# Where the edge-counting units stand between the matmul units of a graph layer: two passes later in the Q loop, and spread by another rule behind the O and neighbour units

## The chip, the cores and the metric

The kernel runs on one core of a Trainium2 chip. The metric is device time in microseconds (us). Before the change the median of three runs is 1108.72 us (1108.17 to 1108.83).

TensorE (PE in the rows) does the matmuls, with its weight loads as PEld. VectorE (DVE) and ScalarE (ACT) take results out of PSUM, the buffer that matmuls write to. GpSimd (POOL) and SyncE (SP) do little here: SP issues the weight loads from memory.

## The reference

A layer of a graph network on 625 nodes with 1024 features and 20000 edges, all in fp32:

```
xn = layernorm(x)
x  = x + sage(xn, src, dst) + linear_attention(xn)
x  = x + moe(layernorm(x))

sage, one layer:  agg = segment_sum(h[src], dst)
                  h @ W_self + (agg / deg) @ W_neigh + b      (two layers, relu between)
attention:        q = softmax(x Wq, features) / 8;  k = softmax(x Wk, tokens)
                  context = k^T v;  out = (q context) Wo + bo     (16 heads of 64)
```

The sum over edges is done as a product with a count matrix C (source node by target node). The kernel builds C from the edge list on the chip. The mixture of experts after it (8 experts, 2 per token, and a shared one) isn't touched by the change.

## The kernel before, in words

**Precision.** Each fp32 product is made of three passes of a "hi" part and a "lo" part: hi*hi, hi*lo, lo*hi (lines 1653 to 1655). Weights are split when they have landed: ScalarE casts `w_hi` (line 688), then VectorE subtracts for `w_lo` (line 996), a quarter of a matrix at a time.

**Units and the ring.** All work of TensorE is cut into units, listed in one order in `units` (lines 97 to 150). Unit number n in that list writes PSUM buffer n mod 4 (`RING = 4`, `slot`). Before a unit starts, `claim` waits until the unit four places ahead of it in the list has been taken out of that buffer. ScalarE or VectorE gives the buffer back (`free`). A unit's place in the list is thus also what decides for whom it waits. Each engine's own program runs in order.

**Names.** In the texts here a unit is called by its kind and number:
- q0 to q9: the query projection of token tile m mod 5, half m // 5, of 24 matmuls. VectorE takes it: maximum (line 1318), subtraction (1323, which gives the buffer back), then ScalarE's exponential (798), VectorE's sum (1327), reciprocal and scaling (1331).
- qt0 to qt9: the transposes of a normalised q tile (line 1692), two passes later (`QLAG = 2`). ScalarE copies them out (802).
- at0 to at4: attention of a token tile (line 1818): 8 matmuls in 16 rows. ScalarE casts `at_hi` (776), VectorE makes `at_lo` (1307) and then gives the buffer back.
- ctx0, ctx1: the attention context (1784).
- o(h,i) and g0(h,i): the output projection and the neighbour projection, half h, token tile i. They are in `mains`, 20 units. VectorE adds the bias to o (1357). For g0 ScalarE casts the hi part (692) and VectorE makes the lo part (1002) and gives the buffer back.
- c0 to c48: counting units. Each is four small matmuls (line 1752) of two one-hot matrices. ScalarE makes `src_oh` (785 four times, then 788), VectorE makes `dst_oh` (1276). VectorE adds the result into C (1288, twice) and gives the buffer back (1290). Three sets of one-hots are kept (`GBUF = 3`): set u+3 is made after unit c(u) is done.
- hs0, hs1, ...: the node's own projection in the first graph layer, after the mains.

**Order of the Q loop.** It has passes m = 0 to 11. TensorE issues q(m), then qt(m-2), then the counts of `Q_COUNTS[m]`, then the at units of `BEHIND_QT[m]` (8: at0, 9: at1, 10: at2, 11: at3 and at4). Before, `Q_COUNTS` puts c0 to c7 in passes 0 to 7, one each. VectorE's pass is: the softmax of q(m); `context` in passes 0 and 1; a weight split in passes 0, 1, 6 and 7; the adding of the pass's count and the next one-hot; the `at_lo`. So a weight split stands ahead of the count's adding. ScalarE's pass is: exponential, copy of qt(m-2), the `w_hi` of passes 0, 1, 6, 7, the `src_oh`, the `at_hi`.

**Order of the mains.** Behind each of the 20 units stand its counts (`behind`): two each, and three behind o(0,3), together 41. Weight splits stand at token tiles 1 and 2 of each half.

Of the kernel before, what the change touches and what calls it, by code (L numbers as in the profile page):

```python
# [5 lines left out]
def gps_layer(nc, x, src, dst, w_self0, w_neigh0, b0, w_self1, w_neigh1, b1,  # L6
# [26 lines left out]
    NT = -(-N // T)  # L33
# [32 lines left out]
    CU = NG // PER  # L66
# [37 lines left out]
    BEHIND_QT = {2 * NT - 2: [0], 2 * NT - 1: [1], 2 * NT: [2], 2 * NT + 1: [3, 4]}  # L104
    for m in range(KF + KLAG - 1):
        units += ([("k", m)] if m < KF else []) + ([("kt", m - KLAG)] if m >= KLAG else []) + ([("perm", m - 1)] if m else [])
    Q_COUNTS = {m: [m] for m in range(2 * NT - QLAG)}
    IN_Q = len(Q_COUNTS)
    BEHIND_Q = {0: [("kt", KF - 1), ("ctx", 0)], 1: [("ctx", 1)]}
    for m in range(2 * NT + QLAG):  # L110
        if m < 2 * NT:
            units += [("q", m)] + BEHIND_Q.get(m, [])
        if m >= QLAG:
            units += [("qt", m - QLAG)]
        units += [("cnt", u) for u in Q_COUNTS.get(m, [])]
        units += [("at", i) for i in BEHIND_QT.get(m, [])]
    mains = [(name, h, i) for name in ("o", "g0") for h in range(2) for i in range(NT)]
    SPLIT_AT = {1: 0, 2: 1}
    behind = {key: 2 for key in mains}
    behind[("o", 0, NT - 2)] += CU - IN_Q - 2 * len(mains)  # L120
    assert behind[("o", 0, NT - 2)] in (1, 2, 3)
    mixed, u = [], IN_Q
    for m, key in enumerate(mains):
        mixed.append(key)
        for _ in range(behind[key]):
            mixed.append(("cnt", u))
            u += 1
    assert u == CU
# [74 lines left out]
    with ctx:  # L203
# [470 lines left out]
        def _(act):  # L674
            copy = nc.scalar.copy

            def wait_unit(key, base=None):
                act.wait_ge(ready[slot(key)], use(key) + 1 if base is None else base * BU + (use(key) + 1))

            def split_hi(job, base=None, quarters=(0, 1)):  # L680

                b = job % 2
                shift = (lambda v, per: v) if base is None else (lambda v, per: base * per + v)
                if job >= 2:
                    wait_unit(last_unit[job - 2], base)
                for s in quarters:
                    act.wait_ge(w_loaded[s], shift(16 * (job + 1), 64))
                    copy(w_hi[b][:, s * HK:(s + 1) * HK, :], w_raw[s][:, :, :]).then_inc(hi_done, 1)  # L688
# [103 lines left out]
            for m in range(2 * NT + QLAG):  # L792
# [13 lines left out]
                if m in Q_SPLITS:  # L806
                    split_hi(Q_SPLITS[m][0], quarters=Q_SPLITS[m][1:])
                for u in Q_COUNTS.get(m, []):
                    wait_unit(("cnt", u))
# [176 lines left out]
        def _(dve):  # L986
# [19 lines left out]
            def wait_unit(key, base=None):  # L1006
                dve.wait_ge(ready[slot(key)], use(key) + 1 if base is None else base * BU + (use(key) + 1))
# [213 lines left out]
            for m in range(KF):  # L1221
                key, b = ("k", m), m % 2
# [90 lines left out]
            for m in range(2 * NT + QLAG):  # L1313
                if m < 2 * NT:
                    key, rows = ("q", m), R(m % NT)
                    q_b = q_s[0:rows, m % 2, :]
                    wait_unit(key)
                    V_.reduce_max(q_m[0:rows, :], heads(PS(key)[0:rows, 0, :]), axis=AX.X)
                    V_.drain()
                    if m >= 2:  # L1320

                        dve.wait_ge(ready[slot(("qt", m - 2))], use(("qt", m - 2)) + 1)
                    V_.tensor_tensor(heads(q_b), heads(PS(key)[0:rows, 0, :]), wide(q_m[0:rows, :]),
                                     ALU.subtract).then_inc(q_sub, 1)
                    V_.drain().then_inc(free[slot(key)], 1)
                    dve.wait_ge(q_expd, m + 1)
                    V_.reduce_sum(q_sum[0:rows, :], heads(q_b), axis=AX.X)
                    V_.drain()
                    V_.reciprocal(q_sum[0:rows, :], q_sum[0:rows, :])
                    V_.drain()  # L1330
                    V_.scalar_tensor_tensor(heads(q_b), heads(q_b), float(DH) ** -0.5,
                                            wide(q_sum[0:rows, :]), ALU.mult, ALU.mult).then_inc(q_done, 1)
                    if m < 2:
                        context(m)
                    if m in Q_SPLITS:
                        split_lo(Q_SPLITS[m][0], quarters=Q_SPLITS[m][1:])
                if m == 0:
                    dve.wait_ge(bin_at_ready, 1)
                    dve.wait_ge(c_cleared, 1)
                bins_at = load_bins(Q_COUNTS.get(m, []))  # L1340
                for u in Q_COUNTS.get(m, []):
                    add_counts(u, bins_at)
                    one_hots(u + GBUF)
                for i in BEHIND_QT.get(m, []):
                    attention_lo(i)
# [92 lines left out]
            for n in range(KF):  # L1438
                if n == HK:
                    split_lo(J_L1)  # L1440
                key = ("h", n)
# [19 lines left out]
            for h in range(2):  # L1461
                split_lo(J_L1 + 2 * h + 1)
                for i in range(NT):
                    key = ("g1", h, i)
# [7 lines left out]
                for i in range(NT):  # L1472
                    key = ("x1", h, i)
# [136 lines left out]
            with dve.Fori(0, blocks) as j:  # L1610
                for h in range(2):
                    split_lo(J_X + h + 1, j)
                    for n in range(h * HK // 2, (h + 1) * HK // 2):
                        key = ("he", n)
# [25 lines left out]
        def _(pe):  # L1640
# [181 lines left out]
            for m in range(2 * NT + QLAG):  # L1822
# [10 lines left out]
                if m >= QLAG:  # L1833
                    n = m - QLAG
                    pe.wait_ge(q_done, n + 1)
                    transposes(("qt", n), lambda a: q_s[0:R(n % NT), n % 2, a * 128:(a + 1) * 128], HK, R(n % NT), R(n % NT))
                for u in Q_COUNTS.get(m, []):
                    count(u)
# [279 lines left out]
```

## Time and profile before

| | |
|---|---|
| median of three runs | 1108.72 us |
| the profiled execution's own time | 1108.72 us |
| its span, first to last instruction | 1106.7 us |
| TensorE busy | 1092.8 us, 99% of the span |
| VectorE, ScalarE busy | 639.7 us (58%), 483.1 us (44%) |
| passes of the Q loop | from 146.73 us (q0) to 230.23 us (start of o(0,0)) |
| mains and their counts | 230.23 to 354.79 us (start of hs0) |
| granted clock | 1.00 |

A timeline row gives the start in us, the duration in us, engine, line, operation, output<-input, shapes, how many are merged, and in brackets how long the engine was idle before it and who released it. Matmul records overlap: the next matmul starts before the record of the one ahead of it ends. So the distance of two starts is the price of a step, and the idle time in brackets understates a stall by the part that the record ahead covers. A weight-load row is a matmul's companion and isn't shown.

### The profile page before, as it was taken

To read this page: it belongs to the slowest core of one execution; us is meant where nothing else is said; L and a number is where in the kernel's file an instruction comes from. 1 tells how busy PE (TensorE), PEld (TensorE's weight loads), DVE (VectorE), ACT (ScalarE), POOL (GpSimd) and SP (SyncE) were. 2 spreads that over 40 slices of the span, in tenths; PEclk is the share of its full clock that TensorE was granted. 3 is DMA by queue.
4 is the path that set the end of the run, shared out by engine and by line. 5 is a ranking of instruction groups with operands and counts; after the bars stand their busy time and mean duration, and the time that the engine had idled before them with its cause. 6 is when DMAs were issued, how large, how long until landed. Compare 5 with 4: busy or idle time off the path is not lost.

```text
span 1106.7 us, 16447 instructions
## 1 busy us (share of the span) xinstructions
PE 1092.8 (99%) x6225; PEld 948.2 (86%) x6225; DVE 639.7 (58%) x880; ACT 483.1 (44%) x712; POOL 67.2 (6%) x88
## 2 busy tenths in 40 slices
PE   7999999999999999999999999999999999999998
PEld 5889998787778999878789999898888988988876
DVE  6889967755666753343474423444746656556556
ACT  4513344557786321301234222245655646555550
POOL 2000000000000000000000530200000000000003
PEclk9999999999999999999999999999999999999999
DMA  7222202213322103622004442477577576766757
GB/s 250 77 77 77 72 9 74 76 58 117 111 77 77 60 19 120 219 76 76 1 1 169 154 111 77 151 258 271 175 270 251 195 277 218 236 228 208 238 182 283
DMA packets 76488, 157.01 MB, mean 142 GB/s; under 512 B 7160, under 2 KB 7432, under 8 KB 76432
## 3 DMA queue, kind: packets, MB, share of 16 engines
q1 hardware_dynamic: 64908, 127.30, 34.0%
q10 hardware_dynamic: 7300, 15.41, 3.8%
q0 software_dynamic: 4224, 13.55, 3.8%
q8 instruction: 36, 0.59, 0.2%
q14 instruction: 20, 0.16, 0.0%
HBM read 135.69 MB, written 20.54 MB: 141 GB/s over the span
## 4 chain that ended last, share of the span: by engine, by line
PE 88%; DVE 4%; ACT 2%; DMA 2%; DVEq 2%; issue 1%; SPq 0%; POOL 0%; ACTq 0%; POOLq 0%
PE ps L1653 21%; PE ps L1655 21%; PE ps L1654 21%; PE ps L2067 10%; PE ps L2068 5%; PE ps L1692 1%; PE ps L1738 1%; PE ps L1970 1%; PE ps L1901 1%; PE ps L1971 1%; PE ps L1902 1%; DVE x L1631 1%; PE ps L1752 1%; ACT src_oh L785 1%; ACT w_hi L688 1%
## 5 line engine op out<-in xcount | busy, mean ns | idle before, releaser
L996 DVE TENSOR_TENSOR w_lo<-w_raw,w_hi 128x2048 fp32r<-128x2048 f32 x108 | 245.2, 2290 | 137.5 <-ACT w_hi L688 135.5
L688 ACT CAST w_hi<-w_raw 128x2048 fp32r<-128x2048 f32 x108 | 203.8, 1911 | 96.6 <-PE ps L1971 36.2
L2067 PE MATMUL ps<-xe,w_hi 128*128 128x448 f32 x512 | 160.9, 375 | 0.0
L2068 PE MATMUL ps<-xe,w_lo 128*128 128x224 f32 x512 | 134.8, 263 | 0.0
L2067 PEld LDWEIGHTS ps<-xe,w_hi 128*128 128x128 f32 x512 | 95.9, 187 | 7.9
L1653 PE MATMUL ps<-w_hi,he_hi 128*128 128x512 f32 (+1 forms) x256 | 101.2, 395 | 0.0
L1655 PE MATMUL ps<-w_hi,he_lo 128*128 128x512 f32 (+1 forms) x256 | 100.2, 391 | 0.0
L1654 PE MATMUL ps<-w_lo,he_hi 128*128 128x512 f32 (+1 forms) x256 | 100.0, 391 | 0.0
L1653 PE MATMUL ps<-w_hi,xt_hi 128*128 128x512 f32 (+1 forms) x240 | 95.9, 400 | 2.1 <-DVEq L1290 2.0
L2068 PEld LDWEIGHTS ps<-xe,w_lo 128*128 128x128 f32 x512 | 97.5, 190 | 0.4
L1655 PE MATMUL ps<-w_hi,xt_lo 128*128 128x512 f32 (+1 forms) x240 | 93.7, 390 | 0.0
L1654 PE MATMUL ps<-w_lo,xt_hi 128*128 128x512 f32 (+1 forms) x240 | 93.6, 390 | 0.0
L1653 PE MATMUL ps<-xt_hi,w_hi 128*128 128x314 f32 x256 | 79.4, 310 | 0.0
L1653 PE MATMUL ps<-t_hi,w_hi 128*128 128x314 f32 x256 | 78.8, 308 | 0.0
L1654 PE MATMUL ps<-t_lo,w_hi 128*128 128x314 f32 x256 | 78.8, 308 | 0.0
L1655 PE MATMUL ps<-xt_hi,w_lo 128*128 128x314 f32 x256 | 78.7, 307 | 0.0
L1655 PE MATMUL ps<-t_hi,w_lo 128*128 128x314 f32 x256 | 78.6, 307 | 0.0
L1654 PE MATMUL ps<-xt_lo,w_hi 128*128 128x314 f32 x256 | 78.6, 307 | 0.0
L785 ACT ACTIVATE src_oh<-iota_c,src_f 128x128 f16<-128x128 bf16 x196 | 62.4, 389 | 20.3 <-DVE o_s L1357 15.3
L1653 PE MATMUL ps<-w_hi,t_hi 128*128 128x512 f32 (+1 forms) x160 | 62.6, 391 | 0.0
L1655 PE MATMUL ps<-w_hi,t_lo 128*128 128x512 f32 (+1 forms) x160 | 62.4, 390 | 0.0
L1654 PE MATMUL ps<-w_lo,t_hi 128*128 128x512 f32 (+1 forms) x160 | 62.4, 390 | 0.0
(324 smaller groups left out, 1986.7 us busy)
## 6 DMA issues: line engine op xcount, KB each, us to landing
w_raw<-in_L_ffn_w SPq DMA_DIRECT2D x64, 1024.0 KB
w_raw<-in_L_gnn_W_neigh SPq DMA_DIRECT2D x8, 1024.0 KB
w_raw<-in_L_gnn_W_self SPq DMA_DIRECT2D x8, 1024.0 KB
w_raw<-in_L_ffn_shared_gate_up SPq DMA_DIRECT2D x8, 1024.0 KB
w_raw<-in_L_mix_Wv SPq DMA_DIRECT2D x4, 1024.0 KB
w_raw<-in_L_mix_Wk SPq DMA_DIRECT2D x4, 1024.0 KB
w_raw<-in_L_mix_Wq SPq DMA_DIRECT2D x4, 1024.0 KB
w_raw<-in_L_mix_Wo SPq DMA_DIRECT2D x4, 1024.0 KB
```

The source lines that it names most:

```text
L688: copy(w_hi[b][:, s * HK:(s + 1) * HK, :], w_raw[s][:, :, :]).then_inc(hi_done, 1)
L785: nc.scalar.activation(src_oh[b][:, c, :], iota_c[:, 0:128, 0], ACT.Abs, bias=src_f[:, g * GC + c:g * GC + c + 1]).then_inc(src_abs, 1)
L996: V_.tensor_tensor(w_lo[b][:, k, :], w_raw[s][:, :, :], as32(w_hi[b][:, k, :]), ALU.subtract).then_inc(lo_done, 1)
L1631: V_.scalar_tensor_tensor(x1[0:R(i), i, :], y_g[c][0:R(i), i, :], wts[0:R(i), c, i:i + 1], x1[0:R(i), i, :], ALU.mult, ALU.add)
L1653: mat(out_ap, lh, rh, start=start, stop=False)
L1654: mat(out_ap, lh, rl, start=False, stop=False)
L1655: return mat(out_ap, ll, rh, start=False, stop=stop)
L1692: last = nc.tensor.transpose(PB(key)[:, a * width:(a + 1) * width], source(a), ident[0:ins, 0:ins])
L1738: last = mat(PB(key)[:, 0:LC], by_place[u % 2][0:rows, n // IL * 128:(n // IL + 1) * 128, n % IL], by_column[u % 2][0:rows, n // IL * LC:( ...
L1752: last = mat(PS(key)[:, a, 0:TD], src_oh[b][:, a * CG + c, :], dst_oh[b][:, a * TD:(a + 1) * TD, c], start=c == 0, stop=c == CG - 1)
L2067: mat(PS(key)[:, a, 0:2 * B], wh[:, k, w_cols], xe[:, :, k, 0:B], start=k == 0, stop=False)
L2068: last = mat(PS(key)[:, a, 0:B], wl[:, k, w_cols], xe_hi[:, k, 0:B], start=False, stop=k == KF - 1)
```

## The change

Two tables of places are made in another way. Nothing is computed differently.

```diff
-    Q_COUNTS = {m: [m] for m in range(2 * NT - QLAG)}
+    Q_COUNTS = {m: [m - QLAG] for m in range(QLAG, 2 * NT)}
...
-    behind = {key: 2 for key in mains}
-    behind[("o", 0, NT - 2)] += CU - IN_Q - 2 * len(mains)
-    assert behind[("o", 0, NT - 2)] in (1, 2, 3)
+    weights_to = [sum(1.75 if key[2] in SPLIT_AT else 2.25 for key in mains[:m + 1]) for m in range(len(mains))]
     mixed, u = [], IN_Q
     for m, key in enumerate(mains):
         mixed.append(key)
-        for _ in range(behind[key]):
+        while u < IN_Q + int((CU - IN_Q) * weights_to[m] / weights_to[-1]):
             mixed.append(("cnt", u))
             u += 1
...
-                if m == 0:
+                if m == QLAG:
                     dve.wait_ge(bin_at_ready, 1)
                     dve.wait_ge(c_cleared, 1)
```

**Q loop.** c0 to c7 now stand in passes 2 to 9, in place of passes 0 to 7. Passes 0 and 1 have none. In passes 8 and 9 a count now stands between qt and at, on TensorE, on VectorE and on ScalarE. VectorE's waits for the cleared C move with the first count.

**Mains.** The number of counts behind each unit, in the order of the units:

| | o(0,0..4) | o(1,0..4) | g0(0,0..4) | g0(1,0..4) |
|---|---|---|---|---|
| before | 2 2 2 3 2 | 2 2 2 2 2 | 2 2 2 2 2 | 2 2 2 2 2 |
| now | 2 2 1 3 2 | 2 2 2 2 2 | 2 2 2 2 2 | 3 1 2 2 3 |

In the rows that follow, `psum_free2` is the semaphore of buffer 2, and line numbers of the changed kernel are lower by 2.

TensorE in pass 8, from qt6 (`ident,q_s`) over at0 (`q_first`, `q_second` with `ctx_s`) to q9 (`w_hi_50,xt_hi`), before:

```order
L1692 MATMUL ps<-ident,q_s 128x128 [waits psum_free1,q_done]
L1692 MATMUL ps<-ident,q_s 128x128 x3
L1818 MATMUL ps<-q_first,ctx_s 128x128 [waits psum_free2,qt_done,ctx_done]
L1818 MATMUL ps<-q_first,ctx_s 128x128 x3
L1818 MATMUL ps<-q_second,ctx_s 128x128 x4
L1653 MATMUL ps<-w_hi_50,xt_hi 113x512 [waits psum_free3]
```

and now:

```order
L1690 MATMUL ps<-ident,q_s 128x128 [waits psum_free3,q_done]
L1690 MATMUL ps<-ident,q_s 128x128 x3
L1750 MATMUL ps<-dst_oh_128,src_oh_131 128x157 [waits src_ready,oh_ready,psum_free0]
L1750 MATMUL ps<-dst_oh_128,src_oh_131 128x157 x3
L1816 MATMUL ps<-q_first,ctx_s 128x128 [waits psum_free1,qt_done,ctx_done]
L1816 MATMUL ps<-q_first,ctx_s 128x128 x3
L1816 MATMUL ps<-q_second,ctx_s 128x128 x4
L1651 MATMUL ps<-w_hi_50,xt_hi 113x512 [waits psum_free2]
```

The count c6 stands ahead of at0, and at0 claims buffer 1, which c5 of pass 7 had; q9 claims buffer 2, which q8 had. Before, at0 claimed the buffer of qt5 and q9 that of the count c7.

VectorE in pass 8, from the maximum of q8 to `at_lo` of at0 and the maximum of q9, before:

```order
L1318 TENSOR_REDUCE q_m<-ps 128x8 [waits psum_ready0]
L1323 TENSOR_TENSOR q_s<-ps,q_m 128x512 [waits psum_ready1]
L1327 TENSOR_REDUCE q_sum<-q_s 128x8 [waits q_expd]
L1329 RECIPROCAL q_sum<-q_sum 128x8
L1331 SCALAR_TENSOR_TENSOR q_s<-q_s,q_sum 128x512
L1307 TENSOR_TENSOR at_lo<-ps,at_hi 128x4x128 [waits hi_out] x2
L1318 TENSOR_REDUCE q_m<-ps 113x8 [waits psum_ready3]
```

and now, from the sum of q8 (its maximum and subtraction stand ahead as before) to `at_lo` of at0:

```order
L1325 TENSOR_REDUCE q_sum<-q_s 128x8 [waits q_expd]
L1327 RECIPROCAL q_sum<-q_sum 128x8
L1329 SCALAR_TENSOR_TENSOR q_s<-q_s,q_sum 128x512
L1294 TENSOR_LOAD bin_at
L1294 ISA x4
L1286 ISA [waits psum_ready0]
L1286 TENSOR_TENSOR c_f<-c_f,ps 128x157
L1286 ISA
L1286 TENSOR_TENSOR c_f<-c_f,ps 128x157
L1274 TENSOR_TENSOR dst_oh_128<-iota_n,dst_126 128x628
L1305 TENSOR_TENSOR at_lo<-ps,at_hi 128x4x128 [waits hi_out] x2
```

The loading of two column offsets, two additions into `c_f` and a one-hot stand ahead of `at_lo`.

TensorE behind g0(1,0), from the first count to g0(1,1) (`w_hi_50,xt_hi`), before:

```order
L1752 MATMUL ps<-dst_oh_128,src_oh_131 128x157 [waits src_ready,oh_ready,psum_free2]
L1752 MATMUL ps<-dst_oh_128,src_oh_131 128x157 x3
L1752 MATMUL ps<-dst_oh_129,src_oh_132 128x157 [waits src_ready,oh_ready,psum_free3]
L1752 MATMUL ps<-dst_oh_129,src_oh_132 128x157 x3
L1653 MATMUL ps<-w_hi_50,xt_hi 128x512 [waits psum_free0]
```

and now:

```order
L1750 MATMUL ps<-dst_oh_130,src_oh_133 128x157 [waits src_ready,oh_ready,psum_free1]
L1750 MATMUL ps<-dst_oh_130,src_oh_133 128x157 x3
L1750 MATMUL ps<-dst_oh_128,src_oh_131 128x157 [waits src_ready,oh_ready,psum_free2]
L1750 MATMUL ps<-dst_oh_128,src_oh_131 128x157 x3
L1750 MATMUL ps<-dst_oh_129,src_oh_132 128x157 [waits src_ready,oh_ready,psum_free3]
L1750 MATMUL ps<-dst_oh_129,src_oh_132 128x157 x3
L1651 MATMUL ps<-w_hi_50,xt_hi 128x512 [waits psum_free0]
```

g0(1,0) itself had buffer 1 before and has buffer 0 now. So g0(1,1) claims the buffer of g0(1,0), where it claimed the buffer of a count ahead of g0(1,0). The same holds for hs0 behind g0(1,4).

## Rows read from the trace of the kernel before

**Rows 1.** The page: TensorE's line of busy time, and its granted clock.
```profile
PE 1092.8 (99%) x6225; PEld 948.2 (86%) x6225; DVE 639.7 (58%) x880; ACT 483.1 (44%) x712; POOL 67.2 (6%) x88
...
PEclk9999999999999999999999999999999999999999
```

**Rows 2.** Waits of TensorE, whole span: who, for whom, total us, times, longest.
```profile
PE ps L1653 <- DVEq L1290: 2.0, 3, 0.9
```

**Rows 3.** Timeline of TensorE near 174 us: start, duration, instruction, idle before.
```profile
173.84 0.45 PE L1752 MATMUL ps<-dst_oh,src_oh 128*128 128x157 f16 x4
175.06 0.50 PE L1653 MATMUL ps<-w_hi,xt_hi 128*128 128x512 f32 x1 [0.77 <-DVEq L1290]
```

**Rows 4.** Timeline of VectorE, same place.
```profile
171.79 2.29 DVE L996 TENSOR_TENSOR w_lo<-w_raw,w_hi 128x2048 fp32r<-128x2048 f32 x1 [0.21 <-issue]
...
174.60 0.32 DVE L1288 TENSOR_TENSOR c_f<-c_f,ps 128x157 f32 x1 [0.17 <-issue]
```

**Rows 5.** Timeline of TensorE, 213 to 231 us.
```profile
213.34 1.06 PE L1818 MATMUL ps<-q_first,ctx_s 128*128 128x128 f32 x8
214.24 1.06 PE L1818 MATMUL ps<-q_second,ctx_s 128*128 128x128 f32 x8
215.58 0.49 PE L1653 MATMUL ps<-w_hi,xt_hi 128*113 128x512 f32 x1 [0.29 <-DVEq L1290]
...
226.67 1.13 PE L1818 MATMUL ps<-q_first,ctx_s 128*128 128x128 f32 x8 [0.17 <-DVEq L1309]
...
230.23 0.48 PE L1653 MATMUL ps<-w_hi,at_hi 128*128 128x512 f32 x1
```

**Rows 6.** Timeline of VectorE, 212 to 226 us.
```profile
212.45 2.29 DVE L996 TENSOR_TENSOR w_lo<-w_raw,w_hi 128x2048 fp32r<-128x2048 f32 x1 [0.82 <-ACT w_hi L688]
...
216.78 0.69 DVE L1323 TENSOR_TENSOR q_s<-ps,q_m 128x512 f32<-128x512 f32 x1
...
221.39 0.69 DVE L1318 TENSOR_REDUCE q_m<-ps 113x8 f32<-113x512 f32 x1 [0.29 <-PE ps L1655]
...
225.19 1.28 DVE L1307 TENSOR_TENSOR at_lo<-ps,at_hi 128x512 fp32r<-128x512 f32 x2
```

**Rows 7.** Timeline of VectorE, one pass of the Q loop with a count.
```profile
175.49 0.69 DVE L1318 TENSOR_REDUCE q_m<-ps 128x8 f32<-128x512 f32 x1
...
181.33 0.69 DVE L1318 TENSOR_REDUCE q_m<-ps 128x8 f32<-128x512 f32 x1
```

**Rows 8.** Timeline of ScalarE at 224 us.
```profile
224.09 1.07 ACT L776 CAST at_hi<-ps 128x512 fp32r<-128x512 f32 x2
```

**Rows 9.** Timeline, 250 to 257 us: TensorE three, ScalarE three, VectorE one.
```profile
254.56 0.75 PE L1752 MATMUL ps<-dst_oh,src_oh 128*128 128x157 f16 x8
256.34 0.45 PE L1752 MATMUL ps<-dst_oh,src_oh 128*128 128x157 f16 x4 [1.03 <-ACT src_oh L788]
256.58 0.47 PE L1653 MATMUL ps<-w_hi,at_hi 128*113 128x512 f32 x1
...
250.61 1.91 ACT L688 CAST w_hi<-w_raw 128x2048 fp32r<-128x2048 f32 x1 [0.27 <-issue]
...
253.73 0.63 ACT L788 ACTIVATE src_oh<-src_oh 128x512 f16<-128x512 f16 x1
...
255.56 0.63 ACT L788 ACTIVATE src_oh<-src_oh 128x512 f16<-128x512 f16 x1
...
255.40 0.69 DVE L1357 TENSOR_TENSOR o_s<-ps,bias_o 128x512 f32<-128x512 f32 x1
```

**Rows 10.** Timeline near 330 us: TensorE, VectorE.
```profile
329.89 0.74 PE L1752 MATMUL ps<-dst_oh,src_oh 128*128 128x157 f16 x8
...
330.70 0.69 DVE L1002 TENSOR_TENSOR n_lo<-ps,n_hi 128x512 fp32r<-128x512 f32 x1 [2.33 <-ACT n_hi L692]
```

**Rows 11.** Timeline of TensorE at the start of the program.
```profile
5.00 4.93 PE L1760 MATMUL ps<-iota_c 128*128 128x392 bf16 x19 [5.00 <-POOLq L588]
...
11.34 1.99 PE L1760 MATMUL ps<-iota_c 128*128 128x392 bf16 x11
```

## The prediction

> **What bounds the kernel now.** I read the page first: TensorE is busy for 1092.8 of 1106.7 us, and the clock row holds 9 in all 40 slices [rows 1]. So the time is TensorE's work plus its stalls. A count that is moved costs the same matmuls wherever it stands; the change is worth only the stalls that it removes or makes. The waits of TensorE come next: in the stretch that the change touches it waited three times for VectorE to give back the buffer of a count, 2.0 us together [rows 2], and once for ScalarE's one-hots [rows 9]. So I then read the timelines at these places, and for each claim in the new order asked when its buffer comes free.
>
> The profiled execution took 1108.72 us, 2.0 us more than its span, and is equal to the median. The sum is made on it. Distances are from start to start; a release reaches TensorE 0.14 us after VectorE's last addition ends (174.60 + 0.32 = 174.92, TensorE at 175.06) [rows 3, 4]. A count alone takes TensorE 0.24 us, two take 0.54, so three take 0.81 (256.34 to 256.58; half of 0.54 for one more) [rows 9]. Where I replay the new order I stay on the old trace's time axis and shift nothing until the end.
>
> **Part 1, the start of the Q loop (c0, c1 out of passes 0 and 1).** q3 should start 0.24 after c2, at 174.08, and started at 175.06: 0.98 lost, waiting for c1, whose adding stood behind the weight split of pass 1 (171.79 to 174.08) [rows 3, 4]. Now q3 claims the buffer of ctx1, which VectorE gives back ahead of that split. The stall goes: **-0.98**. What is late next is nothing: q4 claims c0, which VectorE adds in pass 2, and a pass of VectorE with a count takes 5.84 us (175.49 to 181.33) [rows 7], less than TensorE's own, so it has caught up. The edit to the wait for the cleared C costs nothing, it only moves later.
>
> **Part 2, passes 6 and 7.** q8 claims c4 where it claimed c6. Both are added in pass 6 behind its weight split, so this stall stays: 0.
>
> **Part 3, at0 and q9.** c6 stands ahead of at0, which so wants to start at 213.34 + 0.24 = 213.58 [rows 5]. It claims the buffer of c5, which VectorE adds in pass 7, behind the weight split of 212.45 to 214.74 [rows 6]. In the old trace the count of that pass was released to q9 at 215.58, and VectorE's pass is unchanged. So at0 starts at 215.58: +2.00. It takes 2 * 0.90 = 1.80 (213.34 to 214.24 is its half) and ends at 217.38. q9 claims q8, given back at the end of the subtraction: 216.78 + 0.69 + 0.14 = 217.61 [rows 6], so +0.23. The old stall of q9 goes, 215.58 - (214.24 + 0.90) = 0.44. Together **+1.79**. Behind the waiting at0 stand q9 and all the rest of TensorE's program. q9 starts at 217.61.
>
> **Part 4, passes 8 to 11.** VectorE took up q9 5.81 us after its start (215.58 to 221.39) [rows 5, 6], now at 223.42. Pass 9 now holds a count, so `at_lo` of at1 starts after a whole pass of 5.84 [rows 7], at 229.26, takes 1.28 [rows 6] and ends at 230.54. ScalarE's extra one-hot set doesn't make it later: `at_hi` of at1 stood 2.70 after VectorE's maximum of q9 (224.09 - 221.39) [rows 6, 8] and moves by the 1.83 of a set (253.73 to 255.56) [rows 9]; its first half is ready 5.1 after the maximum, before 5.84. at3 claims the buffer of at1: 230.54 + 0.14 = 230.68. From at3 to the first output unit took 3.56 (226.67 to 230.23) [rows 5], now 234.24. That is 4.01 later than 230.23. Of it 0.48 is the two counts, which are work taken out of passes 0 and 1 and no loss, and 1.79 is part 3. The rest is **+1.74**, stalls at qt9 (which claims c7) and at3. Cover: at4 and its casts move along with at3; the bias load is issued after at4, and the weight loads of SP follow splits that are not reordered. Bounds: nothing lost (0, if `at_lo` kept its old distance to q9), and 3.6 if the two sets of ScalarE, 2 * 1.83, came on the path whole. I take 1.74, from the pass row, since VectorE's chain is the longer one.
>
> **Part 5, behind o(0,3).** Before, the third count c16 should have started at 254.56 + 0.54 and started at 256.34, waiting for a one-hot set ready at 255.56 + 0.63 = 256.19; o(0,4) then at 256.58 [rows 9]. Now o(0,2) has one count, the third one behind o(0,3) is c15, and its set is the one ready at 253.73 + 0.63 = 254.36, in time. What is late next is the buffer: three counts behind a unit make the next unit claim that unit's own buffer. VectorE's split has to wait for `w_hi`, 250.61 + 1.91 = 252.52, ends at 254.81, and the bias addition ends at 255.50, released 255.64. o(0,4) starts there, 0.94 earlier, of which 0.27 is the count that is still to come: **-0.67**. Bounds: 0, if one wait only takes the place of the other, and -1.24, if both are gone (256.34 against 255.10). The replay names both ends of the wait, so I take it.
>
> **Part 6, behind g0(1,0) and g0(1,4).** Each now has three counts, so g0(1,1) claims g0(1,0) and hs0 claims g0(1,4). It wants to start 0.81 after 329.89, at 330.70. VectorE starts the lo part only then, because ScalarE's cast goes ahead, and releases at 330.70 + 0.69 + 0.14 = 331.53 [rows 10]: 0.83 lost. The second place has the same pattern. Together **+1.66**. Bounds: 0, if the lo part came before the third count ended, and 2.0 with a restart of 0.1 to 0.2 each. The last counts end a little later, but the casting of C is wanted only after hs1, 14 us on.
>
> **Sum.** -0.98 + 1.79 + 1.74 - 0.67 + 1.66 = +3.54. After hs0 TensorE waited for one thing only in the rest of the program, so the shift is carried to the end unchanged. 1108.72 + 3.54 = **1112.3 us**.
>
> By the Trainium skill ("Perfetto Trace Analysis", Optimizing Tensor Performance) independent matmul groups rotated through different PSUM banks let the evacuation of one overlap the next group's matmuls. Taken as it stands, part 6 would be 0. The trace agrees for two counts behind a unit (the waits of TensorE name none behind any pair in the mains, which takes 0.54), and limits it for three: the rotation hides an evacuation only if it is shorter than the units ahead of the next use, here 0.81 against 1.64.
>
> **The rivals.**
> - *Faster (the other side).* VectorE gives the moved counts' buffers back in time. Then the stalls of q3 (0.98), q9 (0.44) and c16 (1.24) go and none comes: 1108.72 - 2.7 = 1106.0. For it: VectorE has 42% of its time free. Against it: in pass 7 the split is ahead of c5's adding. It decides at 213.58; the split alone ends at 214.74 [rows 6]. This would need VectorE 2.0 us ahead there.
> - *The Q loop's tail hides the two late counts.* Part 4 is 0: 1110.5. For it: before, the two `at` units behind pass 9 lost only some tenths. Against it: at3's claim hangs on VectorE's pass 9, which is longer by the count.
> - *The counts by three cost nothing.* Part 6 is 0: 1110.6. Against it: rows 10.
> - *The clock falls.* Stalls of up to 2 us follow each other in passes 8 to 11. The same constant matmul took 0.26 us on average at the program's start and 0.18 in its second group [rows 11], 1.44 times; the granted clock reads 1.00 (2.4 GHz) in both. If the 15 us from q9 to the first output unit went by that ratio, 6.6 more: 1118.9. Against it: no dip in any slice after stalls of 1 us [rows 1, 9]. The Trainium skill ("TensorE: Matmul & The Clock Gate", A second HAM failure mode: psum-queue depth-cycling) tells of a kernel in which short waits between groups for PSUM made the clock swing; no stretch of this trace shows it.
>
> **How the numbers follow.** Forecast 0.82 (1112.3); tail hidden 0.06; counts by three free 0.05; faster 0.05; clock 0.02. What a measurement can tell from no change is about 0.2%, 2.2 us. The forecast and the clock are slower by more: 0.84. The two cases of +1.8 and +1.9 are within: 0.11. Faster: 0.05. The range goes from just under the two cases in which one part fails (1110.4) to the forecast with the restarts and half of part 4's upper bound (+1.4), 1113.7.
>
> **What would show it.** In the changed kernel's waits of TensorE: no wait at q3; one of about 1.8 at at0 (line 1816) for a count's adding, one at qt9 of about 0.8 and one at at3 over 1 us; none for one-hots at the third count; one of some 0.6 at each of g0(1,1) and hs0 for the lo part. o(0,0) starts near 232.8 in place of 230.23, hs0 near 358.4 in place of 354.79. A start of o(0,0) before 231 would break parts 3 and 4, and with them the forecast.

## The result: slower, and by more than forecast

| | before | changed |
|---|---|---|
| median | 1108.72 us (1108.17 to 1108.84, 5 runs) | 1115.33 us (1112.98 to 1119.59, 5 runs) |
| ratio of the runs | | 1.0069 [1.0042, 1.0097] |
| profiled execution, span | 1108.72, 1106.7 us | 1114.83, 1112.7 us |

The forecast was 1112.3 us, and 1110.4 to 1113.7 as its range. The direction was right. The time lies 3.0 us above the forecast and outside the range. In most comparisons of this case, for the kernel before too, some runs are 4 us or more longer than the rest.

The changed kernel's page: TensorE's busy time and its granted clock in tenths, for [rows 1].

```profile
PE 1095.3 (98%) x6225; PEld 950.0 (85%) x6225; DVE 639.5 (57%) x880; ACT 482.8 (43%) x712; POOL 68.3 (6%) x88
...
PEclk9999999999999999999999999999999999999999
```

The same 6225 matmuls are busy for 2.5 us longer. Busy time alone doesn't say why: mains_only below, in whose windows the clock never falls, has 1.0 more than the kernel before, since the record ahead of each new stall runs into it. The clock row has slices of 28 us and hides a short fall; the windows further down show one.

TensorE's waits in the changed kernel, whole span (who, for whom, us in total, times, longest), for [rows 2]:

```profile
...
PE ps L1816 <- DVEq L1288: 1.9, 1, 1.9
PE ps L1651 <- DVEq L1002: 1.6, 3, 0.7
PE ps L1651 <- DVEq L1357: 1.4, 1, 1.4
PE ps L1816 <- DVEq L1307: 1.2, 1, 1.2
PE ps L1651 <- DVEq L1288: 0.9, 1, 0.9
PE ps L1690 <- DVEq L1288: 0.7, 1, 0.7
```

From top to bottom: at0 waits for a count's adding; g0(1,1), hs0 and a place of 0.4 that the kernel before has too; o(0,4) for its neighbour's bias addition; at3 for at1; q8 as before; qt9 for a count. No wait for one-hots is left.

TensorE's timeline at q3, at q8, around at0 and q9, and through the loop's tail, for [rows 3, 5]; the last line is VectorE's subtraction of q8:

```profile
173.20 0.45 PE L1750 MATMUL ps<-dst_oh,src_oh 128*128 128x157 f16 x4
173.44 0.47 PE L1651 MATMUL ps<-w_hi,xt_hi 128*128 128x512 f32 x1
...
205.68 0.50 PE L1651 MATMUL ps<-w_hi,xt_hi 128*128 128x512 f32 x1 [0.92 <-DVEq L1288]
...
214.04 1.13 PE L1816 MATMUL ps<-q_first,ctx_s 128*128 128x128 f32 x8 [1.89 <-DVEq L1288]
215.01 1.67 PE L1816 MATMUL ps<-q_second,ctx_s 128*128 128x128 f32 x8
216.33 0.77 PE L1651 MATMUL ps<-w_hi,xt_hi 128*113 128x512 f32 x1
...
217.75 0.63 PE L1651 MATMUL ps<-w_hi,xt_hi 128*113 128x512 f32 x1
218.18 0.63 PE L1652 MATMUL ps<-w_lo,xt_hi 128*113 128x512 f32 x1
...
218.88 0.40 PE L1651 MATMUL ps<-w_hi,xt_hi 128*113 128x512 f32 x1
...
223.02 0.60 PE L1690 MATMUL ps<-ident,q_s 128*128 128x128 f32 x4
...
228.71 0.58 PE L1690 MATMUL ps<-ident,q_s 113*128 113x113 f32 x4 [0.69 <-DVEq L1288]
230.53 1.13 PE L1816 MATMUL ps<-q_first,ctx_s 128*128 128x128 f32 x8 [1.24 <-DVEq L1307]
...
215.14 0.69 DVE L1321 TENSOR_TENSOR q_s<-ps,q_m 128x512 f32<-128x512 f32 x1
```

q3 follows its count after 0.24 us, without a wait: part 1. at0 waits 1.89: part 3. Then the same eight matmuls that take 1.06 in [rows 5] take 1.67, and those of q9 start 0.43 apart (217.75 to 218.18) where 0.23 is usual, until 218.88. So q9 takes 6.69 (216.33 to 223.02) against 5.61 in the kernel before (215.58 to 221.19). Below, qt9 and at3 wait as part 4 has it.

The granted clock in stretches (us, TensorE busy, instructions, clock, DMA share, GB/s), changed kernel:

```profile
213.00:216.00 3.00, 1.96 (x14) 0.88 0.60 140
216.00:219.00 3.00, 3.00 (x11) 0.55 0.54 210
219.00:222.00 3.00, 3.00 (x15) 1.00 0.00 0
```

1.00 is 2.4 GHz and 0.50 would be 1.2 GHz, so TensorE ran most of 216 to 219 us at the lower level. Before, all these stretches read 1.00. The cost: 0.35 in at0's second half and 1.08 in q9, together 1.4. q9 started at 216.33 and was due at 215.98: the halves of at0 stand 0.97 apart, and q8's buffer, which q9 claims, came free at 215.14 + 0.69 + 0.14 = 215.97.

The Trainium skill ("TensorE: Matmul & The Clock Gate", A second HAM failure mode: psum-queue depth-cycling) tells of a matmul loop whose short waits for PSUM made the clock swing. The prediction weighed a fall of the clock and gave it 2 in 100. This trace agrees in part: the clock fell behind a wait for PSUM, but once, for some 3 us, behind a single wait of 1.89, and it didn't swing.

VectorE at the second place, 255 to 260 us, for [rows 9]; then TensorE there and at the two places of part 6:

```profile
256.56 2.29 DVE L994 TENSOR_TENSOR w_lo<-w_raw,w_hi 128x2048 fp32r<-128x2048 f32 x1 [0.70 <-ACT w_hi L686]
259.76 0.69 DVE L1355 TENSOR_TENSOR o_s<-ps,bias_o 128x512 f32<-128x512 f32 x1 [0.91 <-issue]
```

```profile
258.16 1.03 PE L1750 MATMUL ps<-dst_oh,src_oh 128*128 128x157 f16 x12
260.64 0.46 PE L1651 MATMUL ps<-w_hi,at_hi 128*113 128x512 f32 x1 [1.45 <-DVEq L1357]
...
333.94 1.03 PE L1750 MATMUL ps<-dst_oh,src_oh 128*128 128x157 f16 x12
335.55 0.50 PE L1651 MATMUL ps<-w_hi,xt_hi 128*128 128x512 f32 x1 [0.58 <-DVEq L1002]
...
359.16 1.03 PE L1750 MATMUL ps<-dst_oh,src_oh 128*128 128x157 f16 x12
360.87 0.38 PE L1651 MATMUL ps<-xt_hi,w_hi 128*128 128x314 f32 x1 [0.68 <-DVEq L1002]
```

The split had waited for `w_hi`, which part 5 had in its sum. Behind it stand 0.91 us marked "issue", which it had not: before, the split waited for nothing and the bias addition followed at once (255.40) [rows 9]:

```profile
253.14 2.28 DVE L996 TENSOR_TENSOR w_lo<-w_raw,w_hi 128x2048 fp32r<-128x2048 f32 x1
```

Start times by segment, changed less before: q8 -1.63; q8 to o(0,0) +5.50; o(0,0) to o(0,4) +0.19; o(0,4) to hs0 +2.02. Sum +6.08, against +6.11 in time.

### The profile page after: what moved, and what is told of

Read it like the earlier page. It is cut to its first block, busy times and chain, and to the rows that moved or that the text cites. A ratio compares the mean times of both kernels' runs of the same rounds, so it can differ in the third digit from the quotient of the medians.

```text
span 1112.7 us, 16447 instructions
## 1 busy us (share of the span) xinstructions
PE 1095.3 (98%) x6225; PEld 950.0 (85%) x6225; DVE 639.5 (57%) x880; ACT 482.8 (43%) x712; POOL 68.3 (6%) x88
## 4 chain that ended last, share of the span: by engine, by line
PE 90%; DVE 4%; DMA 2%; ACT 2%; DVEq 1%; issue 1%; POOL 0%; SPq 0%; ACTq 0%; POOLq 0%
PE ps L1651 21%; PE ps L1653 21%; PE ps L1652 21%; PE ps L2065 10%; PE ps L2066 5%; PE ps L1690 1%; PE ps L1736 1%; PE ps L1968 1%; PE ps L1899 1%; PE ps L1969 1%; PE ps L1900 1%; DVE x L1629 1%; PE ps L1782 1%; PE ps L1750 1%; ACT w_hi L686 1%
```

## The experiments

Each ran in up to twelve timed runs on one chip beside the kernel before, whose median there was 1108.9 to 1109.1. "Mean clock" is that of a whole run. A fall of 3 us takes about 0.0015 off it, so it shows as 0.998 or 0.999. It doesn't say where in the run the clock fell, and the kernel before too has 0.998 in 11 of its 123 runs, so it is a weaker witness than the windows of a profile. The lowest run is given beside the median.

### Each half of the change alone

q_only has `Q_COUNTS` of the changed kernel and the mains of the one before; mains_only the reverse.

```
-    Q_COUNTS = {m: [m] for m in range(2 * NT - QLAG)}
+    Q_COUNTS = {m: [m - QLAG] for m in range(QLAG, 2 * NT)}
```

> The Q loop's part of the change alone; the mains as before. Theory (stalls by claims, and a clock that falls after the stall of 1.9 us at at0): -0.98 at q3, +1.79 at at0 and q9, +1.74 in the tail, that is +2.5 us: 1111.2 where the granted clock stays at 1.00; in most runs it falls after at0 and the run is 1.5 us or more longer, with a spread between runs of several us as in the changed kernel. Rival (the clock has nothing to do with at0; the mains' stalls bring the spread): all runs within 1 us of 1111.2 and mean clock 1.000 in all.

> The mains' part of the change alone; the Q loop as before. Theory: o(0,4) waits for its own buffer (+0.4 against the old one-hot wait, as the changed kernel's trace shows, where the forecast had -0.67), g0(1,1) and hs0 0.8 each: +2.0 us, 1110.7, all runs within 0.5 us and mean clock 1.000, as no stall is over 1.7 us. Rival (the mains bring the spread): runs from 1110 to 1116 with clocks under 1.

q_only: median 1112.65, lowest 1110.40, no run with a mean clock of 1.000 and six of twelve at 0.998 or less. mains_only: 1110.70, lowest 1110.12, ten of twelve at 1.000. Windows of q_only:

```profile
213.00:216.00 3.00, 2.10 (x11) 0.70 0.64 166
216.00:219.00 3.00, 3.00 (x14) 0.73 0.47 184
...
231.00:234.00 3.00, 3.00 (x18) 0.55 0.02 5
234.00:237.00 3.00, 3.00 (x19) 0.88 0.04 11
...
965.00:968.00 3.00, 3.00 (x13) 0.53 0.88 335
```

mains_only agrees with its expectation in the median; three of its runs lie more than 0.5 above, which it had excluded. q_only has the waits of its sum (1.9, 0.7 and 1.2 at at0, qt9 and at3); its median lies 1.4 above the sum, in the direction of a fallen clock, but its lowest run 0.8 below it, which stays unexplained. The falls belong to the Q loop's part: one behind at0, and in this profile a second behind qt9 and at3. A third stands far from the change, behind a wait of 1.98 us for the experts' weights (the matmul that waited starts at 963.61).

### A stall of a chosen length ahead of at0

Three kernels add one wait of TensorE to the kernel before, at the place where the changed kernel stalls, and move nothing.

```
                 pe.wait_ge(qt_done, NT + i + 1)
+                if i == 0:
+                    pe.wait_ge(lo_done, 14)                 # dose_short
+                    pe.wait_ge(q_sub, 9)                    # dose_long
+                    pe.wait_ge(free[slot(("cnt", 7))], use(("cnt", 7)) + 1)   # dose_count7
```

> The kernel before with one wait more: at0 also waits for the weight split of pass 7 (ends 214.74 in the old trace, at0 wants 213.34), one stall of about 1.5 us. Theory (a fall of the clock needs a single stall near 2 us or more): +1.1 us (the old stall of q9 goes), 1109.8, clock 1.000 in all runs. Rival (stalls near 1 us add up to a fall whenever they stand close): falls in some runs, up to 1112 and more.

> The kernel before with one wait more: at0 also waits for VectorE's subtraction of q8, given at 217.5 in the old trace: one stall of about 4.1 us. Theory (a single long stall brings the fall): +3.7 us for the stall, and the clock falls in every run, 1.5 us or more on top: 1113.9 or more. Rival (the fall needs the several stalls of the changed kernel's passes 8 to 11): 1112.4, clock 1.000.

> The kernel before with one wait more: at0 waits until the count of pass 7 has been added, which is what it waits for in the changed kernel by the ring of buffers. Its stall is about 2.1 us (213.34 to 215.58, less the count), between the 1.5 of dose_short, after which the clock was 1.00 in all runs, and the 4.2 of dose_long, after which it fell in all. Without a fall: +2.2 at at0, -0.3 at q9, 1110.6. Theory A (one stall of about 2 us right behind that of q8 is enough): the granted clock falls below 0.9 at 216 to 222 us in most runs, mean clock under 0.9995, and they take 1 to 3 us more, 1111.5 to 1113.5. Theory B (only the later stalls at qt9 and at3 together with it bring the clock down in the changed kernel): the clock stays 1.00 and the time is 1110.6.

| | stall at at0 | median, lowest us | runs with a mean clock of 0.998 or less |
|---|---|---|---|
| dose_short | 1.5 | 1110.05, 1109.31 | 0 of 12 |
| dose_count7 | 2.3 | 1111.71, 1110.22 | 4 of 12 |
| dose_long | 4.2 | 1114.58, 1113.65 | 12 of 12 |

Windows of dose_long (those of dose_short and of the profiled run of dose_count7 read 1.00):

```profile
216.00:219.00 3.00, 1.30 (x10) 0.93 0.87 322
219.00:222.00 3.00, 3.00 (x12) 0.50 0.06 22
```

A stall by itself can bring the clock down: that of dose_long is a wait added to the kernel before, and nothing else was moved. dose_count7 was a miss for both theories: "most runs" was expected by one, none by the other. Three of its four low-clock runs take 1116.6 us or more, so they may have lost it elsewhere.

### The loop's late counts, one at a time

All three kernels keep six counts, behind passes 2 to 7, as in the changed kernel; two of them have a seventh. The extra counts of the mains stand behind units that are followed by no split.

```
+    Q_COUNTS = {m: [m - QLAG] for m in range(QLAG, 2 * NT - QLAG)}                # loop_2_to_7
+    Q_COUNTS = {2: [0], 3: [1], 4: [2], 5: [3], 6: [4], 7: [5], 9: [6]}           # loop_with_pass_9
+    Q_COUNTS = {2: [0], 3: [1], 4: [2], 5: [3], 6: [4], 7: [5], 8: [6]}           # loop_with_pass_8
```

> The kernel before with six counts in the Q loop, behind passes 2 to 7, as the changed kernel has them there, and none behind passes 8 and 9; third counts behind o(1,0), o(1,4) and g0(1,0), none behind o(0,3). It takes from the changed kernel's Q loop the two late counts alone. Theory A (each wait belongs to its place, as in parts 1, 3 and 4): no wait at q3, 0.9 at q8, nothing at at0, 0.3 at q9, nothing over 0.3 at qt9 and at3, 0.2 at o(1,1) and g0(0,0), 0.6 at g0(1,1); no fall of the clock at 213 to 237 us; 1108.7 - 1.0 - 1.2 + 0.15 + 0.2 + 0.6 = 1107.4. Theory B (moving all six counts two passes later makes VectorE late at the end of the loop whatever stands behind passes 8 and 9): at0 or at3 wait over 1 us, and the time is over 1109.

> As loop_2_to_7, with one count more in the Q loop, behind pass 9 (the changed kernel's second late count, without its first), and without the third count behind g0(1,0). It prices part 4 apart from part 3, and asks whether the loop's tail can bring the clock down by itself. Theory A (part 4 is the count of pass 9 alone): no wait at at0, 0.7 at qt9 and 1.2 at at3; against loop_2_to_7 +1.7 for the tail and -0.6 for g0(1,1): 1108.5 where the clock stays; and since its stalls of 0.7 and 1.2 are each shorter than the 1.5 after which it stayed, the mean clock is 1.000 or 0.999. Theory B (two stalls 1.8 us apart count together for the clock): it falls at 231 to 237 us in most runs, and they take about 1 us more, 1109.5. Theory C (part 4 was the echo of the stall at at0): qt9 and at3 wait under 0.5 each, 1107.0.

> As loop_with_pass_9, with the seventh count behind pass 8 in place of pass 9: the changed kernel's first late count without its second. Against loop_2_to_7 and loop_with_pass_9 it prices part 3 alone, and asks whether the stall at at0, without the later ones, brings the clock down. Theory A (part 3 is a matter of the claim alone): 1.9 at at0, none at q9 over 0.2, under 0.3 at qt9 and at3; lowest runs 1109.7, as those of loop_with_pass_9, since 1.8 there stands against 0.7 + 1.2 here. The clock: its stall (1.9, 0.9 at q8 six us ahead) lies between 1.5, after which the clock stayed, and 2.3, after which 4 of 12 runs had 0.998 or less; so it falls in a third of the runs at most. Theory B (the fall in the changed kernel comes from the stall at at0 and nothing else): a mean clock of 0.998 or less in most runs, as in q_only (all of 12 under 1.000).

TensorE's waits of loop_with_pass_9, then of loop_with_pass_8:

```profile
PE ps L1818 <- DVEq L1309: 1.2, 1, 1.2
...
PE ps L1692 <- DVEq L1290: 0.7, 1, 0.7
```

```profile
PE ps L1818 <- DVEq L1290: 1.9, 1, 1.9
```

Each wait goes with its own count, to a tenth: 1.9 at at0 with pass 8's (part 3), 0.7 and 1.2 at qt9 and at3 with pass 9's (part 4), and neither in loop_2_to_7, where at0 and qt9 don't wait and at3 waits 0.2 as before. Lowest runs: 1107.48, 1109.63 and 1110.03, against 1107.4, 1108.5 and 1109.7 expected. The one of pass 9 missed by a wait that it had not named, 0.7 for a one-hot set in the mains; that of pass 8 has such a wait too, of 1.0. The medians are far higher: 1115.27, 1113.00 and 1114.96. So the waits are read from the profiles, and the times bear on them only by the lowest runs; the long runs come back at the end.

The clock: with pass 8's count nine of twelve runs have a mean clock of 0.998 or less, with pass 9's two of twelve; of the runs under 1113 us, four of six and one of six. Windows of loop_with_pass_8 and of loop_with_pass_9:

```profile
213.00:216.00 3.00, 2.27 (x13) 0.70 0.60 180
216.00:219.00 3.00, 3.00 (x13) 0.73 0.44 170
```

```profile
216.00:219.00 3.00, 3.00 (x15) 1.00 0.46 178
...
231.00:234.00 3.00, 3.00 (x15) 1.00 0.73 236
```

So the stall at at0 brings it down without the later two. My expectation of "a third of the runs at most" was wrong, and theory B held. And dose_count7, with a longer stall there (2.3), kept its clock in most of its runs: four of twelve at 0.998 or less, one of the eight under 1113 us. So it looks as if the length of the stall alone doesn't decide, though twelve runs a kernel are few for that; what else does is open.

### What VectorE did in the 0.91 us ahead of the bias addition

hoist_load loads the next unit's column offsets ahead of the split instead of behind it. load_in_two leaves them in place but loads the third count's two offsets just ahead of its adding. Both are made from mains_only.

```
...
+                if key != mains[-1]:                                               # hoist_load
+                    bins_next = load_bins(counts_behind[mains[mains.index(key) + 1]])
                 if key[2] in SPLIT_AT:
                     split_lo(next_job(key), quarters=(SPLIT_AT[key[2]],))
```

```
-                bins_at = load_bins(counts_behind[key])                            # load_in_two
+                bins_at = load_bins(counts_behind[key][:2])
...
+                    if n == 2:
+                        bins_at += load_bins([u])
                     add_counts(u, bins_at[PER * n:PER * n + PER])
```

> The kernel before with the changed kernel's placing of the counts behind the main units (as mains_only), and in VectorE's program the loading of a unit's column offsets moved ahead of the weight split of the unit before it. It tells what held VectorE between the split of o(0,2) and the bias addition of o(0,3), where mains_only shows 0.91 us of idle time marked issue, and TensorE a wait of 1.7 us at o(0,4). Theory A (the loading of six offsets stands there; my part 5 took it at nothing): the bias addition follows the split at once, as in the kernel before; TensorE's wait at o(0,4) falls from 1.7 to about 0.8; the time is 0.9 below mains_only, 1109.8 against its 1110.7; the waits at g0(1,1) and hs0 stay. Theory B (the idle time belongs to the addition itself, restarting after a split that waited for ScalarE): the gap and the wait of 1.7 stay, and the time is 1110.7.

> As mains_only (the kernel before with the changed kernel's placing behind the main units), with VectorE's six column offsets of a unit with three counts loaded in two parts: four at the unit's start, two ahead of the third adding. hoist_load and five_in_the_loop show the loading of six offsets as 3.2 us of VectorE's sequencer (2.92 and 2.71 idle, with 0.3 beside the instruction before), or 0.53 an offset. Theory A (it is paid by the offset, and hidden as far as the split of 2.29 us lasts): four offsets take 2.1, less than 2.29, so the bias addition follows the split of o(0,2) at once, the wait at o(0,4) falls from 1.7 to 0.8, and about 1 us of idle time stands ahead of the third adding, which nobody waits for; 0.9 less than mains_only, 1109.8. Theory B (it is a fixed price for each loading that follows a waiting split): the gap of 0.9 and the wait of 1.7 stay, 1110.7.

VectorE in hoist_load, then in load_in_two:

```profile
255.70 2.29 DVE L994 TENSOR_TENSOR w_lo<-w_raw,w_hi 128x2048 fp32r<-128x2048 f32 x1 [2.92 <-issue]
257.91 0.68 DVE L1355 TENSOR_TENSOR o_s<-ps,bias_o 128x512 f32<-128x512 f32 x1
```

```profile
252.65 2.29 DVE L994 TENSOR_TENSOR w_lo<-w_raw,w_hi 128x2048 fp32r<-128x2048 f32 x1 [0.69 <-ACT w_hi L686]
254.86 0.69 DVE L1355 TENSOR_TENSOR o_s<-ps,bias_o 128x512 f32<-128x512 f32 x1
...
259.39 0.32 DVE L1286 TENSOR_TENSOR c_f<-c_f,ps 128x157 f32 x1 [0.79 <-issue]
```

hoist_load is a miss that taught most: 1115.43 us (1115.19 to 1116.13, 7 runs), 5.6 more than expected. The bias addition does follow the split at once, so the loading was what stood there. But ahead of the split it takes 2.92 us in the open, and the stall of TensorE at o(0,4) grew from 1.7 to 2.9. The same happened at the other splits, where 1.04 us of loading came into the open, and the wait at g0(1,1) grew from 0.6 to 1.2. All seven runs have a mean clock of 0.998 or less, and the profile shows the fall behind the 2.9:

```profile
258.00:264.00 6.00, 5.21 (x16) 0.72 0.64 218
```

Loading six offsets takes about 3.2 us of VectorE's sequencer: in the changed kernel and in mains_only the bias addition starts 3.20 after the split does, of which 2.29 lay beside the split and 0.91 stood out. load_in_two came out as theory A has it: 1109.99 (lowest 1109.23) against 1110.70 of mains_only, the addition right behind the split, 0.79 idle ahead of the third adding, and 0.48 in place of 1.7 at o(0,4). The two ran beside the kernel before at different times; against it they are 1.1 and 1.6 us longer, so the gain by the medians is 0.4 to 0.7 and not the 0.9 expected, while the waits show 1.2.

The price that it was built on, 0.53 an offset, doesn't hold for fewer than six. VectorE's idle time where a load of four offsets stands open, in hoist_load and in five_in_the_loop:

```profile
283.42 2.29 DVE L994 TENSOR_TENSOR w_lo<-w_raw,w_hi 128x2048 fp32r<-128x2048 f32 x1 [1.04 <-issue]
```

```profile
240.83 0.69 DVE L1357 TENSOR_TENSOR o_s<-ps,bias_o 128x512 f32<-128x512 f32 x1 [1.66 <-issue]
```

Two offsets leave 0.58 to 0.79 idle, four 1.04 or 1.05 where the first of the two counts has an even number, and 1.66 where it has an odd one (c7 here, c9 in one_count_less). The loads of six seen in the open, here and in five_in_the_loop (2.71 idle), all begin with an odd one, c13. In the kernel before the six behind o(0,3) begin with c14, and nothing stood out there. That may be because the split was handed over early, not having to wait for `w_hi` (ready at 252.52, its start at 253.14), or because the load of an even start is shorter; no run tells the two apart.

The Trainium skill ("DMA: Bandwidth & Descriptors", Latency and other measured facts) gives a floor of about 600 ns for a `tensor_load`. The trace agrees: a unit's offsets are one such load, and the shortest here, of two offsets, leaves 0.58 to 0.79 us idle, with a part of it beside the instruction ahead.

### Two versions with fewer stalls

third_count_moved changes only the place of the third count; five_in_the_loop and one_count_less take counts out of passes that hold a split, and put them behind the main units that their expectations name.

```
-    behind[("o", 0, NT - 2)] += CU - IN_Q - 2 * len(mains)
+    for key in (("o", 1, 0),):            # third_count_moved
+        behind[key] += 1
```

```
+    Q_COUNTS = {0: [0], 2: [1], 3: [2], 4: [3], 5: [4]}                            # five_in_the_loop
+    Q_COUNTS = {0: [0], 2: [1], 3: [2], 4: [3], 5: [4], 6: [5], 7: [6]}            # one_count_less
```

> The kernel before with one edit: the third count behind o(0,3) stands behind o(1,0). It tells whether the wait of 1.24 us ahead of o(0,4) belongs to three counts at that place, behind a split, or to three counts anywhere. Theory A (the place: ScalarE's weight rounding and VectorE's split make both late there): the wait for the one-hots goes and behind o(1,0) only 0.1 to 0.2 us come, since the bias addition (0.69 + 0.14) starts at once and three counts take 0.81; time 1108.7 - 1.1 = 1107.6. Theory B (three counts anywhere ask for more one-hots than ScalarE gives): a wait of about 1.2 moves to o(1,0) or o(1,1), and the time is 1108.7.

> The kernel before, with counts in passes 0, 2, 3, 4 and 5 of the Q loop only (none in pass 1, 6 and 7) and third counts behind o(0,4), o(1,0), o(1,4) and g0(1,0), none behind o(0,3). It asks whether the waits of the Q loop come from the passes that hold both a split and a count, as my accounts of q3 and at0 have it. Theory A (they do): the waits at q3, q8 and q9 (2.0 us together) and the one for the one-hots (1.0) go, nothing of 1 us comes at at0, o(1,0), o(1,1) and g0(0,0) wait 0.1 to 0.2 each for their own buffer and g0(1,1) 0.6; 1108.7 - 2.1 - 1.2 + 0.5 + 0.6 = 1106.5, clock 1.00 everywhere. Theory B (VectorE is late in every pass, whatever it holds, since it is the slower engine there): the waits only change their names and the time stays within 0.5 of 1108.7.

> The kernel before without a count in pass 1 of the Q loop (passes 0 and 2 to 7 keep theirs) and with third counts behind o(1,0) and o(1,4) in place of o(0,3). It joins the two gains that the other runs point to, to see whether they add. Theory A (they do): no wait at q3 and none for the one-hots at o(0,3), 0.2 each at o(1,1) and g0(0,0), q8 and q9 as before; 1108.7 - 1.0 - 1.2 + 0.35 = 1106.9, clock 1.000. Theory B (a gain ahead of q8 is lost at q8, because VectorE and not TensorE sets the pace from pass 2 on): q8 and q9 wait 1.0 longer in all, 1107.8.

third_count_moved: 1107.95 (lowest 1107.41), beside 1108.93 (lowest 1108.02), ratio 0.9998 [0.9977, 1.0019]. The wait of 1.0 for one-hots is gone and none came; by the interval it isn't told from no change. It is the lowest median of all kernels here. five_in_the_loop: 1114.05, lowest 1108.50, against 1106.5 expected; one_count_less: 1114.15, lowest 1107.87, against 1106.9. Their waits at q3 went as expected, and in five_in_the_loop those at q8 and q9 too. But each got a wait for a one-hot set in the mains (0.7 and 1.0), and five_in_the_loop 1.2 at o(1,0), where VectorE shows 2.71 idle on issue ahead of o(0,4)'s addition: six offsets again. A stall removed in the loop came back in the mains, where ScalarE's sets are just in time.

### The changed kernel again

> The changed kernel once more, in twelve runs and with a second profile, to divide its distance from the prediction. The terms seen so far: the sum of the prediction (3.5), 1.1 more at o(0,4) for the loading of six offsets, and in the first profile 1.5 for a clock that fell behind at0. Theory A (the clock is the rest): the lowest runs, with a mean clock of 1.000, take 1113.0 to 1113.6; those with 0.998 or less take 1 to 3 more; in the profile the windows of 213 to 237 us show the fall where the mean clock is low. Theory B (late expert weights are the rest, as in loop_2_to_7, whose profile has 2.1 us of waits for w_lo in line 2067): runs with a mean clock of 1.000 too are spread up to 1121, and the profile has such waits.

Median 1114.57 (1112.74 to 1116.56, 12 runs). The three runs with a mean clock of 1.000 take 1112.74, 1112.77 and 1113.77; the nine at 0.998 or less have a median of 1114.75. The second profile shows the fall again, and none of its waits is for `w_lo`:

```profile
213.00:216.00 3.00, 1.80 (x14) 0.94 0.51 128
216.00:219.00 3.00, 3.00 (x10) 0.50 0.57 221
```

Theory A holds, with one run at full clock (1113.77) just above its range. With all 19 runs of both comparisons (7 and 12), five have a mean clock of 1.000 (median 1112.98), 14 have less (median 1115.07). That is 2.1 us between them, where the first profile shows 1.4 for the fall. At full clock the changed kernel takes what the sum gives once the loading is in it: 1108.72 + 3.54 + 1.09 = 1113.35.

## Why the prediction was wrong, step by step

- **Part 1, q3: right.** -0.98 forecast; to q8 the gain is 1.63, of which 0.48 is the two counts, so 1.15.
- **Part 2, q8: right.** 0.92 stays.
- **Parts 3 and 4: right.** The segment from q8 to o(0,0) grew by 5.50: two counts 0.48, forecast 1.79 and 1.74, and 1.43 of the fallen clock, together 5.44. loop_with_pass_8 and loop_with_pass_9 give the two parts each to its own count.
- **Part 5: the mis-sized step of the sum.** "The replay names both ends of the wait, so I take it" was wrong. I took -0.67; it was +0.42 (1.66 lost, 258.98 to 260.64, in place of 1.24). The replay moved the wait for `w_hi` ahead of the split and kept the bias addition right behind it. The loading of six offsets, which VectorE's sequencer does between the two, took 3.20 from the split's start, 0.91 more than the split; the prediction had it at nothing. load_in_two, which loads four there, has no such gap. Error 1.09, outside the bounds of 0 and -1.24.
- **Part 6: right.** 0.58 and 0.68 in brackets, 0.20 each more by the distances of starts (333.94 + 0.81 = 334.75 to 335.55, and 359.97 to 360.87), together 1.70 against 1.66.
- **The rival of the clock: the wrong chance, and no term in the sum.** Both profiles of the changed kernel show the fall, and 14 of 19 runs have a mean clock that fits it; I gave it 0.02. My reason against it was that the clock held after stalls of 1 us [rows 1, 9]; at0's was twice as long, a length the trace of before doesn't hold. Its price was wrong the other way: 15 us at 1.44 times the duration, 6.6 us, where it was about 3 us at 1.9 times (0.43 against 0.23 between starts), 1.4 us. It also blamed the stalls of passes 8 to 11 together; the fall came behind the first of them.
- **The other rivals** fell: no stall was hidden that the sum had counted.

For the profiled run the account closes: 3.54 + 1.09 + 1.43 = 6.06, against 6.11 measured. The median of the result lies 0.5 above that run. So of the miss of 3.0 us, 1.1 is the loading, 1.4 the clock, and 0.5 is in nothing that a trace shows. The "would show it" list held, but for o(0,0) (234.10, forecast 232.8), which is late by the clock, and hs0 (360.87, forecast 358.4), late by the clock and the loading; the wait of 1.4 at o(0,4) for the bias addition isn't on the list. Two parts in which nothing was misread, 3 and 4, made most of the forecast, so the right direction is no luck.

Open: why the clock seems to fall more often behind the 1.9 us of pass 8's count than behind the 2.3 of dose_count7. A stall at another time with the same neighbours was not tried.

## What to carry to other kernels

In a ring of buffers a unit's place decides for whom the fourth one behind it waits, so read each move for the claim it makes. A stall of nearly 2 us of TensorE may cost the clock as well (here 1.4 us): add that to the price, and give it a chance of its own when the trace holds no stall so long. When VectorE has loads of registers between two instructions, they are hidden only beside what was handed over ahead of them; once that instruction waits for a semaphore, the loads can come out behind it.

## What the runs showed of the hardware

- Loading registers from memory holds VectorE back, in the open if no long instruction is running: 0.58 to 0.79 us idle for two values, 1.04 to 1.66 for four, 2.71 (five_in_the_loop) and 2.92 (hoist_load) for six. The price isn't proportional to the number.
- In profiles the clock fell behind stalls of 1.9 us (at at0 in four profiles, of three kernels, and once behind 1.98 elsewhere), 2.9 and 4.2 us, and came back after some 3 us. Behind one of 1.5 the profile shows none, and no run of twelve has 0.998 or less. For 2.3 us see above.
- Long runs, most of them at full clock: loop_2_to_7 had nine of twelve above 1111.7, the kernel before six of 35 beside it above 1112. In loop_2_to_7's profile (1111.76) TensorE waits for the experts' weights, which the kernel before doesn't in its profile, and ScalarE, which casts them, waits longer for their landing. TensorE's wait first, then ScalarE's from 750 us on:

```profile
PE ps L2067 <- DVE w_lo L996: 2.1, 3, 0.9
...
ACT w_hi L688 <- DMA w_raw<-in_L_ffn_w: 44.4, 28, 3.0
```

In the kernel before that last line reads 25.9 us, with 1.9 as the longest. Why removing stalls 600 us earlier made such runs more frequent was not settled.
